# Macaron block (MoE, RWKV-style scan, MoE) on one core: value rows for the state scan read back from DRAM instead of spread by TensorE, and four scans in five slots

## What is computed

```
x = x + 0.5 * ffn(layernorm(x))      # 8 experts, top 2, C=128, F=512
x = x + attn(layernorm(x))
x = x + 0.5 * ffn(layernorm(x))

def attn(x):                         # x: (2, 1024, 128)
    ...                              # token shift, low-rank mixes
    r, k, v, g, w = ...              # w = -exp(...)
    def step(S, inp):                # per head: K=16 by V=32 state
        q_t, k_t, v_t, w_t = inp
        kv = k_t[..., :, None] * v_t[..., None, :]
        o_t = einsum('bhk,bhkv->bhv', q_t, S + u[None, :, :, None] * kv)
        S = exp(w_t)[..., None] * S + kv
        return S, o_t
    _, o = scan(step, S0, (r, k, v, w))      # 1024 steps, 4 heads
    o = per-head normalise(o) * gn_weight + gn_bias
    return (o * silu(g)) @ W_o.T
```

## Time and profile before

| | us |
|---|---|
| median of 3 runs | 531.13 (530.73 to 532.26) |
| the profiled execution, its own time | 532.41 |
| its span, first to last instruction | 530.6 |
| PE busy | 512.0 (96%) |
| DVE busy | 388.5 (73%) |
| ACT busy | 304.5 (57%) |
| POOL busy | 201.3 (38%) |
| DMA | 25.70 MB, mean 48 GB/s |

### The profile page before, as it was taken

How to read it: one execution, slowest core, us unless ns; L and a number is a source line. 1 busy time by engine, 2 the same in 40 slices (tenths; PEclk the granted TensorE clock), 3 DMA queues, 4 the chain that set the end, 5 groups by cost and what they waited for, 6 DMA issues and landing times.

```text
span 530.6 us, 6194 instructions
## 1 busy us (share of the span) xinstructions
PE 512.0 (96%) x1946; PEld 320.0 (60%) x1946; DVE 388.5 (73%) x745; ACT 304.5 (57%) x481; POOL 201.3 (38%) x228
## 2 busy tenths in 40 slices
PE   7999999999999999999989999999999999999996
PEld 3566575565557545555745555566655557777774
DVE  3555388688849698886998899679789968784443
ACT  2766587642367654335775633288552338787773
POOL 0025421657611253763105276501527741112212
PEclk9999999999999899999999999999999999999999
DMA  6184111011101002010003011001101111003200
GB/s 227 52 296 183 40 41 40 3 40 41 40 0 41 1 1 80 40 41 1 2 1 119 2 41 40 17 25 41 60 2 40 40 41 55 6 1 119 61 0 20
DMA packets 10352, 25.70 MB, mean 48 GB/s; under 512 B 2640, under 2 KB 2768, under 8 KB 10192
## 3 DMA queue, kind: packets, MB, share of 16 engines
q1 hardware_dynamic: 10320, 25.32, 14.2%
HBM read 24.13 MB, written 1.18 MB: 48 GB/s over the span
## 4 chain that ended last, share of the span: by engine, by line
PE 48%; issue 21%; POOL 13%; DVE 12%; ACT 3%; DMA 1%; POOLq 0%; SPq 0%; DVEq 0%; ACTq 0%
PE Y L282 11%; PE U L261 7%; POOL qs L805 6%; PE U L263 6%; PE U L262 6%; POOL xT L789 4%; PE Y L277 3%; PE Y L278 3%; PE Y L279 3%; DVE hid_lo L655 3%; DVE pool_a L708 2%; DVE gy L664 1%; DVE xnt L590 1%; DVE aw L736 1%; POOL pool_a L811 1%
## 5 line engine op out<-in xcount | busy, mean ns | idle before, releaser
L484 ACT ACTIVATE hid<-U,small 128x512 f32<-128x512 f32 x152 | 104.4, 687 | 140.7 <-PE U L263 140.1
L789 POOL TENSOR_TENSOR xT<-xT,gy 128x512 f32<-128x512 f32 x64 | 83.7, 1308 | 228.3 <-DVE gy L664 228.1
L282 PE MATMUL Y<-hid,w 128*128 128x512 f32 x304 | 155.0, 591 | 0.0
L261 PE MATMUL U<-xhi,w1lo 128*128 128x512 f32 x256 | 140.6, 549 | 2.5 <-ACT hid L484 1.5
L655 DVE TENSOR_TENSOR hid_lo<-hid,hid_hi 128x512 fp32r<-128x512 f32 x104 | 77.4, 752 | 33.5 <-ACT hid_hi L482 32.9
L263 PE MATMUL U<-xhi,w1hi 128*128 128x512 f32 x256 | 101.0, 394 | 0.0
L262 PE MATMUL U<-xlo,w1hi 128*128 128x512 f32 x256 | 100.9, 394 | 0.0
L481 ACT ACTIVATE hid<-U,small 128x512 f32<-128x512 f32 x104 | 71.4, 687 | 42.0 <-PE U L263 37.7
L805 POOL TENSOR_TENSOR qs<-q,pool_a 128x512 f32<-128x512 f32 x64 | 75.9, 1187 | 27.4 <-DVE pool_a L691 27.4
L261 PEld LDWEIGHTS U<-xhi,w1lo 128*128 128x128 f32 x256 | 48.3, 189 | 55.0 <-issue 38.5
L482 ACT ACTIVATE hid_hi<-U,small 128x512 fp32r<-128x512 f32 x104 | 71.0, 682 | 0.0
(11 more groups left out here) (127 smaller groups left out, 554.6 us busy)
## 6 DMA issues: line engine op xcount, KB each, us to landing
G<-gate_dram SPq DMA_DIRECT2D x32, 512.0 KB, 3.8
pool_a<-wexp_dram SPq DMA_DIRECT2D x8, 256.0 KB, 5.4
w<-wexp_dram SPq DMA_DIRECT2D x8, 256.0 KB, 5.5
xT<-xT_dram SPq DMA_DIRECT2D x4, 256.0 KB, 6.2
qs<-const_dram SPq DMA_DIRECT2D x1, 1024.0 KB, 10.3
out_dram<-xT SPq DMA_DIRECT2D x4, 256.0 KB, 4.3
small<-small_dram SPq DMA_DIRECT2D x1, 656.0 KB, 8.3
gate_dram<-gate_T SPq DMA_DIRECT2D x32, 4.0 KB, 1.4
```

The source lines that it names most:

```text
L261: mm(dst, w1lo[:, e, f, :], xhi[:, k % NB, :], start=True, stop=False)
L282: mm(dst, w2[:, g % E, f, :], hid[:, n % HS, :], start=first, stop=final).then_inc(down, 1)
L484: act.activation(hid[:, n % HS, :], U[n % 2][:, :], ACT.Relu, bias=bias).then_inc(h_f, 1)
L789: pool.tensor_tensor(xT[:, h, b, :], xT[:, h, b, :], gy[:, g % 2, :], ALU.add).then_inc(acc, 1)
```

## The change

ACT copies the values whole as `v` (no `vlo`). SP writes `v` to DRAM twice over (`v_dram`, each row doubled, `VD` = 2), waits for both, and issues the first five of 16 fetches: each reads 8 value rows so that every one stands on 16 partitions (`value_rows`), 256 KB into one of five SBUF tiles `vb`. ACT issues the other eleven, each behind the multiply that frees its tile. DVE multiplies `vb` by `kk`, both in SBUF, into the PSUM bank. `v_spread`, `sel`, its 1 MB load and its cast are gone. Scans start at t = 18 and stand in four of every five slots (t = 18 to 36), `reduce` at t = 24, 29, 34, 39, the group norm from t = 40, `T_OUT` at t = 48. The stretch without parts runs from t = 15 to 47 (t = 13 to 33 before): 68 slots of 256 are in parts instead of 104. `PREP` moves the blocks 4 to 7 by 5, 4, 3 and 4 slots. SP's queue is written by slot: the broadcasts into `G` are issued one by one at `gates_slot`, and the weights of experts 4 to 7 no longer stand behind block 0's fourth broadcast.

```diff
-PREP = [None, 6, 34, 80, 114, 125, 167, 208]
+PREP = [None, 6, 34, 80, 119, 129, 170, 212]
...
 HS, QS, SS = 5, 8, 4
-FP, PS, GS = 3, 3, 6
+FP, PS, GS, VS = 3, 3, 6, 5
+VD = 2
 
...
-T_XM, T_Z, T_MUS, T_PR, T_SC = 5, 7, 9, 12, 16
-T_PO = T_SC + VG + 2
-T_VAR, T_NORM, T_OUT = T_PO + 2, T_PO + 3, T_PO + 10
+T_XM, T_Z, T_MUS, T_PR, T_SC = 5, 7, 9, 12, 18
+SC = 20
+T_PO = T_SC + SC + 2
+T_VAR, T_NORM, T_OUT = T_PO + 2, T_PO + 3, T_PO + 8
 MIX = (1, 0, 2, 3, 4)
-MUS_BANK, SPREAD_BANK = (0, 1, 2, 0, 1), (1, 2, 0)
+MUS_BANK, STATE_BANK = (0, 1, 2, 0, 1), (1, 2, 0)
...
+def gates_slot(k, c):
+
+    if k == 0 and c < GS // EQ:
+        return -1
+    return max(4 * (k * E + (c + 1) * EQ - GS) + 4, PREP[k] + T_RT + 5 if k else 0)
+
+
+def scan_at(t):
+
+    j = t - T_SC
+    return 4 * (j // 5) + j % 5 if 0 <= j < SC and j % 5 < 4 else None
+
...
-    scans = any(start + T_SC - 3 <= n < start + T_PO for start in UNIT)
+    scans = any(start + T_SC - 3 <= n < start + T_OUT for start in UNIT)
...
+        v = sb("v", [P, NT])
+        vb = sb("vb", [P, VS, NT])
...
+
+            def gates_in(k, c):
+                at = (k * E + c * EQ) % GS
                 sp.wait_ge(g_out[k], 64)
+                if k * E + (c + 1) * EQ > GS:
+                    sp.wait_ge(comb, k * E + (c + 1) * EQ - GS)
                 rows = gate_dram[k // NB].rearrange("(b k e t) p -> b k (e t p)", b=NB, k=NQ, e=EQ)
-                for k4 in range(NQ):
-                    at = (k * E + k4 * EQ) % GS
-                    if k * E + (k4 + 1) * EQ > GS:
-                        sp.wait_ge(comb, k * E + (k4 + 1) * EQ - GS)
-                    sp.dma_start(G[:, at:at + EQ, :].rearrange("p e n -> p (e n)"),
-                                 rows[b, k4].partition_broadcast(P)).then_inc(g_in[at // EQ], 16)
+                sp.dma_start(G[:, at:at + EQ, :].rearrange("p e n -> p (e n)"),
+                             rows[k % NB, c].partition_broadcast(P)).then_inc(g_in[at // EQ], 16)
+
+            def values(i):
+                sp.wait_ge(v_r, i + 1)
+                for d in range(VD):
+                    sp.dma_start(v_dram[i].rearrange("(r d) n -> r d n", d=VD)[:, d, :], v[:, :]).then_inc(v_out[i], 16)
+                sp.wait_ge(v_out[i], 16 * VD)
+                for m in range(VS):
+                    n = i * VG + m
+                    if n >= VS:
+                        sp.wait_ge(kv_r, n - VS + 1)
+                    sp.dma_start(vb[:, n % VS, :], value_rows(v_dram[i], m)).then_inc(v_in[n % VS], 16)
...
+            for c in range(GS // EQ):
+                gates_in(0, c)
...
-            sp.dma_start(sel_raw, const_in[:, C_SEL:C_ALL]).then_inc(sel_l, 16)
...
-            gates_to_rows(1)
-            for k in range(2, 6):
-                gates_to_rows(k)
-            for k in (6, 7):
-                rows_out(k - 2)
-                gates_to_rows(k)
+            for n in range(ALL):
+                for k in range(1, BLOCKS):
+                    if n == PREP[k] + T_RT + 5:
+                        gates_to_rows(k)
+                for k in range(BLOCKS):
+                    for c in range(NQ):
+                        if n == gates_slot(k, c):
+                            gates_in(k, c)
+                for i in range(UNITS):
+                    if n == UNIT[i] + T_PR + 1:
+                        values(i)
+                for k in (4, 5):
+                    if n == (k + 1) * SLOTS + 8:
+                        rows_out(k)
...
-            def v_spread(i, m):
-                if m >= 3:
-                    pe.wait_ge(st_r, i * VG + m - 2)
-                elif m == 0:
-                    pe.wait_ge(sel_r, 1)
-                    pe.wait_ge(vlo_r, i + 1)
-                    pe.wait_ge(bet_c, i + 1)
-                elif m == 1:
-                    pe.wait_ge(bv_r, i + 1)
-                else:
-                    pe.wait_ge(sg_r, i + 1)
-                dst, j = A[SPREAD_BANK[m % 3]][:, :], order(m)
-                mm(dst, sel[:, j, :], vlo[:, :], start=True, stop=False)
-                mm(dst, sel[:, j, :], vhi[:, :], start=False, stop=True).then_inc(vb, 1)
...
-                if T_SC <= t < T_SC + VG:
-                    v_spread(i, t - T_SC)
-                if T_SC + 5 <= t < T_SC + 5 + VG and (t - T_SC - 5) % 4 == 0:
-                    reduce(i, (t - T_SC - 5) // 4)
+                if T_SC + 6 <= t <= T_SC + SC + 1 and (t - T_SC) % 5 == 1:
+                    reduce(i, (t - T_SC) // 5 - 1)
...
+            def fetch(i, m):
+                n = i * VG + m
+                act.wait_ge(kv_r, n - VS + 1)
+                act.dma_start(vb[:, n % VS, :], value_rows(v_dram[i], m)).then_inc(v_in[n % VS], 16)
...
+                m = scan_at(t - 1)
+                if m is not None and m + VS < VG:
+                    fetch(i, m + VS)
...
-                    act.activation(vhi[:, :], A[2][:, :], ACT.Copy).then_inc(vhi_r, 1)
+                    act.activation(v[:, :], A[2][:, :], ACT.Copy).then_inc(v_r, 1)
...
-                bank = A[SPREAD_BANK[m % 3]][:, :]
-                dve.wait_ge(vb, n + 1)
-                dve.tensor_tensor(bank, bank, kk[:, :], ALU.mult).then_inc(kv_r, 1)
+                bank = A[STATE_BANK[m % 3]][:, :]
+                dve.wait_ge(v_in[n % VS], 16 * (n // VS + 1))
+                dve.tensor_tensor(bank, vb[:, n % VS, :], kk[:, :], ALU.mult).then_inc(kv_r, 1)
...
-                if t == T_PR + 1:
-                    dve.wait_ge(vhi_r, i + 1)
-                    dve.tensor_tensor(vlo[:, :], A[2][:, :], vhi[:, :], ALU.subtract).then_inc(vlo_r, 1)
                 if t == T_PR + 2:
+                    dve.wait_ge(v_r, i + 1)
...
-                if T_SC <= t < T_SC + VG:
-                    scan(i, t - T_SC)
+                if scan_at(t) is not None:
+                    scan(i, scan_at(t))
...
-                if n == SLOTS:
-                    dve.wait_ge(sel_l, 16)
-                    dve.tensor_copy(sel[:, :, :].rearrange("p j n -> p (j n)"), sel_raw).then_inc(sel_r, 1)
...
-                if T_SC <= t < T_SC + VG:
-                    m = t - T_SC
+                m = scan_at(t)
+                if m is not None:
                     read_state(i, m)
...
+def value_rows(v_dram, m):
+
+    j = order(m)
+    return v_dram[VD * RH * j:VD * RH * (j + 1)].rearrange("(r a) n -> r a n", a=1).to_broadcast([VD * RH, KD // VD, NT])
```

29 lines of the change are left out of this document (12 added, 17 removed).

## The result

The changed kernel takes 518.63 us (median of four runs, 518.23 to 518.85) against 531.09 (530.73 to 532.26) of the kernel before on the same chip: 0.9761 of it, 95% interval 0.9744 to 0.9778. That is 12.5 us, more than twice the 5.6 that were forecast, and inside the range. The profiled execution's span went from 530.6 to 516.6.

What follows compares the result with a forecast made beforehand. PE and DVE were taken to have the same pace in the scans, PE setting it elsewhere. -37.0 + 6.1 + 9.7 + 4.0 + 9.4 + 1.7 = -6.1 us; forecast 525.5 us, 8-in-10 range 511 to 539.

Steps and rivals of the forecast that it cites:

- The clock: At the reduces of units 2 and 3: longer PE waits bring one fall of the granted clock, +1.7 us, bounds 0 and +6.8.
- Six slots and parts: Over all four units: last reduce six plain slots earlier, -37.0 us; 36 slots go from parts to plain, +6.1.
- First multiply later: Start of each unit's scans: first multiply waits for a 9.0 us trip over DRAM, not PE's spread; +9.7 us, bounds +3.7, +23.
- From first multiply to last reduce: Scans of each unit: DVE sets the stretch, 37.9, 38.65, 40.8 and 40.65 us against 38.5 before; +4.0 us.
- the port: DVE's multiply, two SBUF operands: waits for POOL once behind each of 18 combines, 0.52 us each; +9.4, bounds 0 and +33.
- Routing between the first scans: DVE in units 2 and 3: routing steps moved between the first scans, 1.9 us and 1.0 us, within the +4.0.
- Waits on ACT: ACT's fetch issues in the scans: waiting for a multiply holds relus back, but PE waits at a reduce anyway; costed at nothing.
- Rival A: Scans PE-paced: multiply rarely meets POOL, DRAM trip short (7.5 us); -23 us, 508 to 509, singly 510 to 518; chance 0.17.
- Its check: Whole kernel: PE alone would give 30.7 less 6.1, so the six slots can never yield more than 24.6 us.
- Rival B: Scans: POOL is always in an instruction when a multiply comes; 549 us with all 64 colliding, 531 to 540 with half; chance 0.20.
- C: Trip over DRAM of 12 us (+12) or two more clock falls (+3.4): 531 to 540 us; chance 0.13 together with D.
- D: Scans: PE's spread was covered anyway, so the fifth slot is lost; inside C's range of 531 to 540; chance 0.13 with C.

## Why the prediction was right in direction and too small

The spans differ by 14.0 us, the sum said 6.1. The direction and the exchange that the sum is built on, slots gained against time given back, were right. Two terms failed. The clock was put at +1.7 for a fall that didn't come, while the fall of before that went was left out: 3.4 us. And the first multiply was priced by a trip over DRAM of 9.0 us, which took 6: 2.6 us on balance. By the sum's own terms:

**Six slots and parts (-37.0 + 6.1 = -30.9).** Measured -33.2, as what remains between and around the units. The method, to count the slots by which the last `reduce` moves, was right to 2.3 us, and 1.7 of these are the fall of the earlier trace rows, which is gone. I read that stretch, and used it only as the price of one more fall. That it was a gain to be had if the slots around it moved was a step that I left out. That parts relieve DVE between the units also was only half seen.

**First multiply later (+9.7, measured +7.1).** The step that failed is the trip of 9.0 us, and with it the idea that the trip is what the first multiply waits for. A write of 256 KB lands in 2.2 us, not in the 4.3 of the output's write. In the timeline of unit 1 (ACT's copy, SP's two writes and five fetches, the `combine` and the first multiply):

```profile
190.27 0.60 ACT L550 ACTIVATE v<-A 128x512 f32<-128x512 f32 x1 [0.37 <-PE A L377]
```

```profile
190.89 0.80 SPq L231 DMA_DIRECT2D v_dram<-v  x2
...
193.59 3.09 SPq L237 DMA_DIRECT2D vb<-v_dram  x5
```

```profile
196.02 0.74 DVE L689 SCALAR_TENSOR_TENSOR gy<-Y,small,G 128x512 f32<-128x512 f32 x1
196.86 1.85 DVE L708 TENSOR_TENSOR A<-vb,kk 128x512 f32<-128x512 f32 x1
```

The first fetch is issued at 193.59 and lands 3.24 us later, at 196.83, which is 6.0 us after the end of the copy; in the other units it is 6.4, 6.2 and 5.8. In unit 1 that is just when the `combine` ahead of the multiply ends (196.76), so the multiply starts 0.8 us earlier after its copy than it did before. In unit 0 the data have landed 1.1 us before the multiply, which stands behind a `combine` that waited for PE. In units 2 and 3 the multiply comes 10 us after the copy because DVE's own routing lies ahead of it, and the kernel with the tables alone, which has no trip, has the same 10.05 and 9.83. So the trip was 3 us too long in the sum, which four times over is 12 us, and the place of the first scan in DVE's order, which the sum doesn't have, took back some 9 of them: that the term came as near as 2.6 us is luck. "Each further microsecond of the trip costs four" was wrong with it: a trip 2 to 3 us longer cost 3.7 us in all, in units 0 and 1 alone. I had priced a chain of transfers without asking what else the first multiply waits for.

**From first multiply to last reduce (+4.0) and the port (+9.4), together +13.4, measured +12.1.** The sum is near, and both of its parts were off; that they cancel is luck. *Pace:* 2.02 us was taken as DVE's from the earlier trace rows. It was PE's: DVE followed the spread. Free of it, multiply and scan are 1.91 us apart (1.97 with `carry`), which is 64 x 0.11 = 7.0 us less. *The port:* one collision for each of the 18 `combine`s was right; there are 19, with the first multiply of unit 1. Their size was not: 13.0 us over the median, 0.69 each and not 0.52. The 0.52 came from L655, which meets POOL's instructions at any point of them; the multiply behind a `combine` in the scans always meets a product that has just begun, 0.36 us before it in units 0 and 1 and 0.48 in units 2 and 3. In the rows of unit 1 above the product takes 1.28 us; the multiply waits for the 0.92 that are left of it and is done 0.56 later. That and the routing steps below make +3.6 and +2.8, so with the -7.0 the three corrections come to -0.6, and -1.3 was measured.

This is what the Trainium skill's page SBUF — State Buffer, section "SBUF: two separate sides", says of the shared port pair, and the trace agrees: the one that starts first keeps it. The PSUM operand confirms it by taking every long multiply away. In the rival I had read the rule as a wait for all of the product's 1.09 us. That is too much for this place, since the multiply starts 0.36 or 0.48 us into it; the rest of the product, 0.6 to 0.9 us, is what the rule gives there, and the 0.69 of the trace's mean agrees.

*Routing between the first scans:* 2.9 us forecast, 5.7 measured (2.0 in unit 2's first gap, 1.7 in its second, 1.9 in unit 3's). The forecast's 1.9 came from a place where POOL was elsewhere. In the timeline of the kernel after, DVE and POOL, first ahead of unit 2's first multiply, then in its first gap, then in unit 3's:

```profile
291.58 1.29 POOL L809 TENSOR_TENSOR xT<-xT,gy 128x512 f32<-128x512 f32 x1 [6.01 <-DVE gy L689]
291.63 0.19 DVE L659 TENSOR_REDUCE rs<-rt 128x4 f32<-128x32 f32 x1
291.85 1.06 DVE L660 TENSOR_TENSOR rt<-rt,rs 128x32 f32<-128x32 f32 x1
...
295.39 1.27 POOL L825 TENSOR_TENSOR qs<-q,pool_a 128x512 f32<-128x512 f32 x1 [2.28 <-DVE pool_a L716]
295.42 1.29 DVE L664 TENSOR_TENSOR rt<-const,rs 128x32 f32<-128x32 f32 x1
...
387.50 1.27 POOL L825 TENSOR_TENSOR qs<-q,pool_a 128x512 f32<-128x512 f32 x1 [4.28 <-DVE pool_a L716]
...
387.72 1.08 DVE L670 TENSOR_SCALAR rs<-rs 128x4 f32<-128x4 f32 x1
```

An instruction of 32 columns takes 1.06 and 1.29 us and ends 0.04 or 0.05 behind POOL's, where its neighbours take 0.19. One of four columns, which reads a single SBUF tensor, takes 1.08 (0.90 in unit 2's second gap) and ends 0.03 behind, where its median is 0.17. They wait for POOL as the multiplies do, and I had counted collisions for the multiplies only.

**Waits on ACT (nothing).** PE was found waiting for ACT in the scans, which I had named as a sign of a wrong forecast. It cost nothing on balance, for another reason than the one given: it spread a stand that would otherwise have cost clock (521.7 with the fetch a slot later; 513.5 with the later fetch and the clock kept, against 513.9 with the earlier one).

**The clock (+1.7).** No fall came, and the one of before went: 3.4 us. That longer waits bring falls was right in mechanism: in the three kernels that let them grow, all six stands at a first `reduce` of 4.1 to 5.2 us came with 6.8 us at half clock. That the waits at the `reduce`s of units 2 and 3 would be of that kind was wrong, by the ACT wait just told.

**In sum**, of the 7.9 us between sum and measurement, 3.4 are the clock, 2.6 the trip, 1.3 the scans and 0.6 a rest that isn't accounted for. Rival A, PE-paced, happened in part: the trip is short, and the 510 to 518 that the prediction gives for only some of its three steps is close to the 518.6 measured. Its check, at most 24.6 us by PE alone, stands. Rival B fell: DVE keeps winning outside the `combine`s. C and D fell as well.

**Open:** single falls of 3.4 us near 272 to 286 us are in the profiles of six of the variants and not in those of the others. Just there PE stands 2.2 us for DVE's `xnt` in every kernel with the new tables, with a fall behind it or without. In the timeline of PE and by windows, the kernel after, then the one with the PSUM operand and the later preparation:

```profile
275.87 0.65 PE L331 MATMUL A<-const,xnt 128*128 128x128 f32 x4 [2.21 <-DVE xnt L615]
```

```profile
275.90:279.30 3.40, 3.40 (x14) 1.74 (x15) 2.29 (x3) 2.68 (x4) 2.59 (x2) 1.00 0.37 94
```

```profile
272.31 0.88 PE L332 MATMUL A<-const,xnt 128*128 128x128 f32 x4 [2.20 <-DVE xnt L618]
```

```profile
272.60:276.00 3.40, 3.40 (x9) 0.99 (x8) 2.03 (x3) 2.71 (x4) 2.59 (x2) 0.50 0.39 142
```

The stand is the same, and only the second is followed by the fall; what decides it stays open. What a POOL free of DVE's routing would bring in units 2 and 3 wasn't tried.
